# Moving the down projection of a fused SSM and FP4 feed-forward kernel in front of the gathering of states, and its norm and output to later slots

## What is computed

```python
u = silu(conv3(x)); B, C = split(u @ W_bc + b_bc); dt = softplus((u @ W_dt + b_dt) @ W_dtp + b_dtp)
h[l] = exp(A * dt[l]) * h[l-1] + B[l] * u_or_x[l] * dt[l]      # a scan over l, for 128 channels x 16 states
x1 = layernorm(x + sum_n(C[n] * h[n]) + x * Dcoeff)
hidden = silu(q(x1) @ q(w_gate).T) * (q(x1) @ q(w_up).T)       # q: blocks of 16, FP4 codes times a scale
out = layernorm(x1 + q(hidden) @ q(w_down).T)
```

## Time and profile before

| what | value |
|---|---|
| time, median of 3 runs | 410.14 us (409.21 to 410.53) |
| time of the profiled execution | 411.21 us |
| its span, first to last instruction | 409.4 us |
| mean granted TensorE clock, share of full | 0.859 |
| busy: DVE, PE, POOL, ACT | 333.6, 284.3, 281.5, 216.1 us |

### The profile page before, as it was taken

How to read it: one execution, slowest core, us unless ns; L and a number is a source line. 1 busy time by engine, 2 the same in 40 slices (tenths; PEclk the granted TensorE clock), 3 DMA queues, 4 the chain that set the end, 5 groups by cost and what they waited for, 6 DMA issues and landing times.

```text
span 409.4 us, 3984 instructions
## 1 busy us (share of the span) xinstructions
PE 284.3 (69%) x1136; PEld 133.2 (33%) x1136; DVE 333.6 (81%) x374; ACT 216.1 (53%) x493; POOL 281.5 (69%) x168
## 2 busy tenths in 40 slices
PE   5478665677866784789397848778578765664783
PEld 2125111212412333334242325233333342234363
DVE  2828969799999999699978999699969998445880
ACT  2634663765575566465927482756546364133235
POOL 0003555568487997499929994799749995976652
PEclk9656698889969996999889996999699668598698
DMA  2470280081018005410261008100530000000001
GB/s 39 109 169 0 52 181 1 0 186 44 2 44 189 0 2 114 92 51 2 51 155 52 0 2 189 48 19 2 126 80 27 0 0 26 1 2 1 26 2 51
DMA packets 19246, 21.86 MB, mean 53 GB/s; under 512 B 6096, under 2 KB 15128, under 8 KB 19224
## 3 DMA queue, kind: packets, MB, share of 16 engines
q1 hardware_dynamic: 19224, 21.60, 23.2%
HBM read 2.72 MB, written 2.10 MB: 12 GB/s over the span
## 4 chain that ended last, share of the span: by engine, by line
PE 31%; POOL 27%; ACT 13%; issue 11%; DVE 11%; SPq 4%; DMA 2%; POOLq 0%; DVEq 0%; ACTq 0%
POOL product L654 8%; PE ps_f L1151 5%; PE ps_b L1111 5%; POOL qh_norm L675 4%; POOL qh_norm L670 4%; DVE states L862 4%; PE ps_prep L1089 4%; PE ps_y L1069 3%; DVE db L849 3%; PE ps_prep L1104 3%; PE ps_f L1149 2%; SPq L412 2%; POOL rstd L664 2%; POOL xq L694 2%; POOL qx_norm L675 2%
## 5 line engine op out<-in xcount | busy, mean ns | idle before, releaser
L654 POOL TENSOR_TENSOR product<-states,c_rep 128x1024 f32<-128x1024 f32 x64 | 150.7, 2360 | 60.3 <-DVE states L862 57.1
L450 ACT ACTIVATE ps_decay<-dt_rep,aneg 128x512 f32<-128x512 f32 x128 | 87.0, 693 | 38.2 <-DVE states L862 38.1
L862 DVE TENSOR_TENSOR_SCAN states<-ps_decay,states,db 128x512 f32<-128x512 f32 x64 | 79.9, 1263 | 14.1 <-POOL product L654 9.5
L849 DVE SCALAR_TENSOR_TENSOR db<-ps_b,bbc_rep,dt_rep 128x2048 f32<-128x2048 f32 x32 | 74.8, 2338 | 11.7 <-PE ps_b L1111 9.4
L862 DVE TENSOR_TENSOR_SCAN states<-ps_decay,db 128x512 f32<-128x512 f32 x64 | 76.3, 1207 | 8.6 <-issue 4.6
L1104 PE MATMUL ps_prep<-u_feat,wbc_rep 128*128 128x512 f32 x64 | 39.5, 701 | 22.5 <-ACT c_rep L516 19.4
L1111 PE MATMUL ps_b<-u_feat,wbc_rep 128*128 128x512 f32 x64 | 43.3, 765 | 16.4 <-DVE db L849 16.4
L1069 PE MATMUL ps_y<-product,gather 128*32 128x512 f32 x256 | 39.1, 687 | 6.0 <-POOL product L654 5.7
L1136 PE MATMUL ps_f<-gate_t,xq_t 128*128 128x352 f32 x64 | 30.1, 554 | 14.5 <-DVE hidden L916 8.9
L516 ACT ACTIVATE c_rep<-ps_prep,bbc_rep 128x512 f32<-128x512 f32 x32 | 22.1, 692 | 28.2 <-PE ps_prep L1104 28.2
L662 POOL TENSOR_TENSOR var_eps<-var,eps 128x4 f32<-128x4 f32 x16 | 3.5, 220 | 45.8 <-ACT hq_t L524 39.3
(11 more groups left out here) (150 smaller groups left out, 505.1 us busy)
## 6 DMA issues: line engine op xcount, KB each, us to landing
dt_rep<-dtx SPq DMA_DIRECT2D x128, 128.0 KB, 2.4
x_tok<-in_L_attn_x SPq DMA_DIRECT2D x8, 256.0 KB, 3.0
out<-y_out SPq DMA_DIRECT2D x8, 256.0 KB, 2.3
hidden<-in_L_ffn_w_down SPq DMA_DIRECT2D x1, 176.0 KB, 2.5
x_feat<-in_L_attn_x SPq DMA_DIRECT2D x8, 0.5 KB, 2.7
hidden<-in_L_ffn_w_gate SPq DMA_DIRECT2D x1, 128.0 KB, 2.2
hidden<-in_L_ffn_w_up SPq DMA_DIRECT2D x1, 128.0 KB, 2.2
alog<-in_L_attn_A_log SPq DMA_DIRECT2D x4, 8.0 KB
```

What stands on the lines that cost most here:

```text
L450: nc.scalar.activation(ps_decay[BANK_OF[k]][:], dt_rep[p][:, c, 0, :], ACT.Exp, scale=aneg[:, c, m:m + 1]).then_inc(decay_done, 1)
L654: nc.gpsimd.tensor_tensor(product[:, j % PRODUCTS], states[p][:, first:first + 2, :], over(c_rep[p][:, j // SET_PAIRS, :], 2), ALU.mult).t ...
L849: nc.vector.scalar_tensor_tensor(out=db[m % DB][:], in0=over(ps_b[:], QUADS), scalar=bbc_rep[:, 0, m:m + 1], in1=dt_rep[p][:, :, 1, :], op ...
L862: nc.vector.tensor_tensor_scan(out=states[p][:, k % ring, :], data0=ps_decay[BANK_OF[k]][:], data1=db[k // QUADS % DB][:, k % QUADS, :], i ...
```

## The change

`AT` loses the second slot of the down projection on TensorE, so that all four tiles are done in slot 6, in front of `spread_b` (m = 3) and `sum_states` (m = 0). GpSimd's norm of the down projection goes from slot 8 to slot 11, where it stands behind product 5, and ScalarE's y_out from slot 11 to slot 13, where it stands behind the evacuation of xq and in front of the decay and the tanh of slot 14. The variance stays in slot 8. The tail's order is written out in `tail` and does not change. No instruction is added or removed.

```diff
-    "pe sum": (7, 11, 15, 2), "pe r": 3, "pe xq": 13, "pe tiles": 14, "pe hq": 3, "pe down": (6, 7),
+    "pe sum": (7, 11, 15, 2), "pe r": 3, "pe xq": 13, "pe tiles": 14, "pe hq": 3, "pe down": (6,),
...
-    "act variance": 8, "act y": 11,
+    "act variance": 8, "act y": 13,
...
-    "pool r norm": 4, "pool x norm": 8, "pool xq": 10, "pool h norm": 6, "pool norm": 8,
+    "pool r norm": 4, "pool x norm": 8, "pool xq": 10, "pool h norm": 6, "pool norm": 11,
```

## The result

The changed kernel takes 417.77 us (median of 4 runs, 416.45 to 419.55), beside 410.33 us for the kernel before on the same chip (median of 4, 409.21 to 411.11): ratio 1.0186, 95% interval 1.0141 to 1.0232. In a second set on another chip it took 419.01 us (median of 5) beside 410.55, ratio 1.0192, 1.0162 to 1.0222. It is slower by about 7.5 us. The forecast was 414.8 us, with a range up to 417.5: the sign and the chain of waits came out, the size did not, and the time lies 0.3 us outside the range.

A forecast was written before the change was run, and what follows sets the result against it. ScalarE was taken to lose 39.9 us in five waits for the down projection's second half. Losses of 2 x 1.05 (steps 3, 5), 1.4 (4), 0.55 (6), 0.65 (7) make 4.7: 410.14 + 4.7 = 414.8 us, range 411.0 to 417.5.

The forecast's parts named there:

- Projection and B: TensorE, slots 6 and 7: the projection ends at 253.6, 2.8 us sooner; B ends at 254.6, 1.9 us later.
- D: Zero point of each step: TensorE's restart with the down projection in slot 6, at 247.18 in step 5 before.
- Product 4 and L821: GpSimd's product 4 goes at 256.6; VectorE's L821 on x1 waits it out until 259.2; code arithmetic only 0.7 us sooner.
- y_out and the up product: Slot 13: rstd, there at 267.7, holds y_out, so the up product goes at 268.95, 1.85 us late.
- From the up product to the second gate tile: TensorE, step 5: 2.54 us, taken from gapless step 4, puts the second gate tile at 271.5, 1.3 us late.
- Rival C: TensorE's clock rises later than before behind its restart, up to 1 us a step: up to 417.5 us; chance 0.03.
- The even step, 6 and 7, and the cover of store and load: Next D 1.4 us late in step 4, 0.55 in 6, 0.65 in 7; store and load covered with 2.3 us.
- L821 first (B): VectorE's L821 on x1 comes before product 4, and L823 meets that product instead: 412.2 us; chance 0.09.
- the cancelling (D): VectorE's idle 2.21 us absorbs more of the late hidden tiles; gains and losses cancel: 410.1 us; chance 0.09.
- Rival A: VectorE's L821 on x1 keeps its short 0.42 us, not held by product 4: 406.4 us, faster; chance 0.15.

The follow-up runs named there:

- e8: Changed kernel with VectorE's L821 and L823 on x1 moved from slot 10 to slot 9, only in steps 3 to 7: 405.94 us.
- e1: Changed kernel with the norm back in slot 8 and y_out back in slot 11, leaving only the whole projection in slot 6: 405.02 us.
- e10: Changed kernel with GpSimd's norm back in slot 8, y_out staying in slot 13: 407.50 us, ratio 0.9938 to the kernel before.
- e4: Changed kernel with two needless TensorE products added in the wait for y_out, steps 3 to 6: 414.43 us.
- e5: Changed kernel with GpSimd's norm in slot 10, in front of product 5, instead of slot 11: 413.25 us.

## Why the prediction was right in kind and wrong in size

- **Projection and B: right.** The projection ends 6.0 us behind D (256.26 - 250.24) where 6.4 was forecast, B 6.9 us where 7.4 was forecast. In step 5 the clock rises 0.4 to 0.5 us sooner than assumed, and all that follows lies that much earlier against D. In the steps 4 and 6 it does not: product 4 goes at D + 9.6 and D + 9.5, where 9.4 was forecast. ScalarE's waits for L1151 are 5.6 us at most; about 5.5 was forecast.
- **Product 4 and L821: right.** Both sit where they were put, 0.28 us apart (0.3 forecast), L821 takes 2.36 us (2.3 forecast), the code arithmetic starts at D + 13.0 (13.5), rstd is there at D + 20.1 (20.5). It holds in all five steps with a down projection: L821 takes 2.23 to 2.36 us in the steps 3 to 7 and 0.41 to 0.57 in the three others; before, 0.41 to 0.55 in all eight. e8, without the meeting, is 12 to 13 us faster.
- **y_out and the up product: right.** TensorE idles 1.78 to 1.85 us for y_out, and the up product is 1.4 us late against D in step 5, the 1.85 less the 0.45 from the clock's earlier rise.
- **From the up product to the second gate tile: wrong, and this is the step that failed.** The prediction took 2.54 us from the earlier trace rows, a stretch at the higher clock, and carried it into a stretch in front of which its own sum had put 1.85 us of idle time. Measured are 4.28 us in steps 3 and 5, and 2.65 in step 4. The second gate tile of step 5 comes at D + 25.6 in place of D + 24.3, 1.3 us more, and the next D is 1.3 us later than forecast (2.34 against 1.05). In step 3 it is 1.7 us (2.74 against 1.05). Those two terms are the 3.0 us by which the 7.7 of the trace exceeds 4.7. In step 5 the miss would have been larger by the 0.45 of the earlier rise, which hid a part of it by chance. Rival C had the clock in view, but in slot 6 and as a rise that comes late; the fall was in slot 14, and so the price sat in no case and the range ended 0.3 us too low.
- **The even step, 6 and 7, and the cover of store and load: right.** 1.61 against 1.4, 0.49 against 0.55, 0.51 against 0.65. The reader of x, L1080, has no new wait for a DMA.
- **Rivals.** L821 first (B) and the cancelling (D) did not occur. Rival A's rule does not hold, but its price nearly does: e8, in which the two do not meet, takes 405.94 us, forecast 406.4. The terms lie elsewhere, so this is luck in part: its steps 3 to 7 are 1.0, 0.3, 0.4, 2.5 and 1.2 us shorter than before, where 0.55, 0.35, 0.55, 1.2 and 1.1 were priced. What should have been weighed there is what e1 shows: the norm in slot 8 costs nothing once the projection is whole, and leaves 0.35 us of spare time. Then it would have been plain that the gain lay in the first edit, and that the norm's late place turned it into a loss (407.50 us with the norm back in slot 8, e10).

## What to carry to other kernels

When a reordering makes an engine wait where it used not to, do not only shift the work behind the wait, but price it at the clock that the idle time may leave, and give that case a chance of its own. An instruction that stood behind a wait (here the norm in front of product 4) has to be costed anew when the wait moves: it may have become free exactly where it is. And two edits that each gain can lose together, if one spends the time in hand on which the other relies; time each alone.

## What the runs showed of the hardware

- TensorE's clock after short idle times. Behind 1.85 us without work in step 5, B took 1.91 us and the gathering 1.47; behind 1.78 us in step 4, 1.02 and 1.07. From the first C product to the up product both stretches show the same rows with the same lengths; in front of the first C they differ, as the clock had risen later behind D in step 4 (product 4 at D + 9.6 against D + 8.9). The second profile has the same pattern: behind 1.84 and 1.83 us (steps 3, 5) B took 1.91 us, behind 1.79 and 1.78 (steps 4, 6) 1.02. With 0.60 to 0.68 us (e4) or 0.17 us (e5, e8, e10) of idle time it stayed at the higher clock in each of the steps 3 to 6. The length of the idle time does not decide it alone: in the last stretch of the changed kernel the gathering at 369.17 took 1.06 us behind 2.02 us of idle time, and in e1 the one at 317.57 took 1.94 behind 1.66. What does is left open.
- The exclusion is complete and picks its instructions. L821 went from 0.42 to 2.36 us and L823 from 0.26 to 2.32 when a product of GpSimd had started 0.28 us before. It holds the other way round too: in step 5 of the changed kernel L821 on hidden started at 252.07 and took 0.88, and GpSimd's L683, which started 0.09 us behind it, took 1.70 instead of 1.05. So these two engines do not meet at semaphores alone. db, which has an input in PSUM, keeps its 2.35 us beside a whole product (in e1, db of slot 14 from 261.48, product 5 from 261.56), and so does a scan with its 1.27 (in the changed kernel from 248.49, inside GpSimd's L700 from 246.94 to 249.53). The Trainium skill (GPSIMD Engine Reference, § 1. Specifications) names a contention between the two engines; the runs agree, and give its size: the short instruction ends 0.29 us (L821) or 0.16 us (L823) behind the end of the long one.
